# Collecting three scan directions in one order: where the third direction's products are put back into image order

## The reference

```python
y_f = mamba_dir(xz, ...)                                   # pixels in order
y_b = flip(mamba_dir(flip(xz, -1), ...), -1)               # pixels backwards
xz_s = xz.reshape(b, 2*D_INNER, NSLICES, m).swapaxes(-1, -2).reshape(b, 2*D_INNER, l)
y_s = mamba_dir(xz_s, ...)                                 # third direction: pixels in sliced order
y_s = y_s.reshape(b, D_INNER, m, NSLICES).swapaxes(-1, -2).reshape(b, D_INNER, l)
y = y_f + y_b + y_s
```

## Time and profile before

| what | value |
|---|---|
| median of three runs | 746.49 us |
| the profiled execution, span | 750.81 us, 749.0 us |
| scan layer, six tiles | 298.3 to 601.1 us of the span |
| busy share of the whole span | TensorE 81%, VectorE 86%, ScalarE 68%, GpSimd 57% |
| mean granted TensorE clock | 0.935 |

### The profile page before, as it was taken

One profiled execution on the slowest core, in us unless ns is written; L12 is line 12 of the kernel. 1 busy time (PEld: TensorE's weight loads), 2 busy tenths in 40 slices (PEclk: granted clock), 3 DMA queues, 4 the chain that ended last, 5 costly groups with the idle time before them and its releaser, 6 DMA issues.

```text
span 749.0 us, 11674 instructions
## 1 busy us (share of the span) xinstructions
PE 609.9 (81%) x3947; PEld 349.8 (47%) x3947; DVE 647.5 (86%) x896; ACT 509.2 (68%) x608; POOL 427.3 (57%) x292
## 2 busy tenths in 40 slices
PE   7899998999988952577776777776757888799997
PEld 5655546677764310244443544454435653233332
DVE  7798996889976979999999899999998874788876
ACT  2658531879976767697886796888868611477673
POOL 3699993000001075798898798798986911533331
PEclk9999999999999985699998797999987999999999
DMA  2004200331001031000000000000000013100000
GB/s 58 4 13 97 37 1 8 71 95 24 4 3 60 14 84 39 1 1 0 1 1 0 1 0 1 0 1 1 0 1 0 1 46 56 42 1 0 15 1 14
DMA packets 28853, 14.98 MB, mean 20 GB/s; under 512 B 23022, under 2 KB 24942, under 8 KB 28654
## 3 DMA queue, kind: packets, MB, share of 16 engines
q1 hardware_dynamic: 27582, 13.61, 8.2%
q10 hardware_dynamic: 1216, 0.66, 0.4%
HBM read 5.14 MB, written 0.78 MB: 8 GB/s over the span
## 4 chain that ended last, share of the span: by engine, by line
PE 38%; DVE 36%; ACT 11%; issue 9%; POOL 4%; DMA 0%; DVEq 0%; SPq 0%; ACTq 0%; POOLq 0%
PE ps L588 35%; DVE arena L1397 15%; DVE ps L1069 8%; ACT arena L1639 3%; DVE arena L1069 3%; DVE arena L1115 2%; POOL arena L1800 2%; ACT arena L1753 2%; DVE ps L1115 1%; DVE arena L1284 1%; PE ps L649 1%; PE ps L770 1%; DVE arena L1348 1%; ACT arena L1740 1%; ACT ps L1740 1%
## 5 line engine op out<-in xcount | busy, mean ns | idle before, releaser
L588 PE MATMUL ps<-arena 128*32 128x64 f32 (+5 forms) x2072 | 338.4, 352 | 110.9 <-ACT arena L1753 33.6
L588 PEld LDWEIGHTS ps<-arena 128*32 128x32 f32 (+4 forms) x2072 | 123.4, 123 | 243.4 <-issue 96.2
L1800 POOL TENSOR_TENSOR arena<-arena 128x1024 f32<-128x1024 f32 x91 | 181.7, 2011 | 33.1 <-DVE arena L1397 14.4
L1397 DVE TENSOR_TENSOR_SCAN arena<-arena,ps 128x1024 f32<-128x1024 f32 x60 | 137.2, 2287 | 8.2 <-DVE ps L1069 0.5
L1785 ACT ACTIVATE arena<-ps,nycol 128x1024 f32<-128x1024 f32 x64 | 71.2, 1115 | 56.9 <-PE ps L588 56.9
L1069 DVE TENSOR_TENSOR ps<-arena,ps 128x1024 f32<-128x1024 f32 x69 | 83.8, 1214 | 9.0 <-PE ps L588 8.3
L1397 DVE TENSOR_TENSOR_SCAN arena<-ps,arena 128x1024 f32<-128x1024 f32 x36 | 81.6, 2267 | 0.1
L1740 ACT ACTIVATE arena<-arena,a_col 128x1024 f32<-128x1024 f32 x60 | 68.7, 1144 | 10.1 <-DVE arena L1397 9.7
L1924 POOL TENSOR_TENSOR arena<-arena,bmask 128x128 f32<-128x128 f32 x64 | 30.9, 485 | 77.9 <-PE ps L588 66.8
L1069 DVE TENSOR_TENSOR arena<-ps,arena 128x512 f32<-128x512 f32 (+2 forms) x75 | 48.6, 654 | 24.5 <-PE ps L588 19.7
L1639 ACT ACTIVATE arena<-arena 128x256 f32<-128x256 f32 x128 | 59.0, 504 | 6.1 <-DVE arena L1284 4.7
(11 more groups left out here) (209 smaller groups left out, 1021.0 us busy)
## 6 DMA issues: line engine op xcount, KB each, us to landing
arena<-arena SPq DMA_DIRECT2D x54, 64.0 KB
arena<-arena SPq DMA_DIRECT2D x12, 128.0 KB, 3.3
w_conv<-in_c_far SPq DMA_DIRECT2D x1, 1152.0 KB, 5.7
w_conv<-rpb_pad SPq DMA_DIRECT2D x36, 28.0 KB, 1.8
arena<-x SPq DMA_DIRECT2D x12, 64.0 KB, 2.0
arena<-x1t SPq DMA_DIRECT2D x12, 64.0 KB, 2.0
arena<-x3t SPq DMA_DIRECT2D x12, 64.0 KB, 2.0
arena<-arena SPq DMA_DIRECT2D x2, 288.8 KB, 3.7
```

Source lines behind the costliest of these rows:

```text
L588: return pe.matmul(o, l, r, start=start, stop=stop, **k)
L1397: ve.tensor_tensor_scan(hs_ring[n % RING], decay, add, 0.0, ALU.mult, ALU.add).then_inc(S("scan"), 1)
L1800: return gp.tensor_tensor(o, a, b, ALU.mult)
```

## The change

GpSimd's products of the third direction are written in image order. The states and C are read in sequence as before, and the output is addressed so that neighbours in the sequence land 64 elements (256 bytes) apart. All three directions of a pair then add up in one sum. `turn_back` at the tile changes 0 to 1 and 3 to 4, `collect_third` and both ScalarE copies for them are gone, and so are two items of the ring (102 items are left of 104). The skip term of tiles 0 and 3 is written in image order as well, by ScalarE, with a read in steps of 16 elements. The counts of the semaphores `y_turned` and `y_back` follow. No wait is added.

```diff
 ITEMS = [(k, what) for k in range(DP) for n in range(NS)
-         for what in ["third"] * (k % DIRS == 1 and n == 0) + ["skip"] * (n == SKIP_AT) + [n]]
+         for what in ["skip"] * (n == SKIP_AT) + [n]]
...
                 collect(hc_ring[item(k, n) % RING], first=(k % DIRS == 0 and n == 0),
-                        last=(k % DIRS != 1 and n == NS - 1), halves_of=end)
+                        last=(k % DIRS == DIRS - 1 and n == NS - 1), halves_of=end)
...
-            def collect_third(k):
-
-                p = k // DIRS
-                pe.wait_ge(S("y_natural"), p + 1)
-                collect(hc_ring[item(k, "third") % RING], first=True)
...
-                    if k % DIRS == 1 and n == 0:
-                        pe.wait_ge(S("y_turned"), 1 + 2 * (k // DIRS))
-                        turn_back(ORDER[k - 1], 6)
                     if k * NS + n + AHEAD < DP * NS:
                         spread(*divmod(k * NS + n + AHEAD, NS))
-                    if k % DIRS == 1 and n == 0:
-                        collect_third(k)
...
-                    if n == 3 and k in (1, DIRS, DIRS + 1):
+                    if n == 3 and k == DIRS:
                         ac.wait_ge(S("y_acc"), above(item(k - 1, NS - 1) + 1))
-                        copy_y(0 if k == DIRS else ORDER[k - 1], slice(0, T))
-                    if n == 4 and k % DIRS == 1:
-                        q = item(k, "third")
-                        ac.wait_ge(S("y_back"), 2 * (k // DIRS + 1))
-                        ac.wait_ge(S("y_acc"), above(q - RING + 1))
-                        ac.activation(hc_ring[q % RING].rearrange("p (s m) -> p s m", s=SLICES),
-                                      bank2(6).rearrange("p (m s) -> p s m", s=SLICES), ACT.Copy).then_inc(S("y_natural"), 1)
+                        copy_y(0, slice(0, T))
...
-                        ac.activation(hc_ring[q % RING], u[:, t // PAIRS, t % PAIRS, ::step], ACT.Copy,
+                        to, of = hc_ring[q % RING], u[:, t // PAIRS, t % PAIRS, ::step]
+                        if k % DIRS == 0:
+                            to, of = to.rearrange("p (s m) -> p s m", s=SLICES), of.rearrange("p (m s) -> p s m", s=SLICES)
+                        ac.activation(to, of, ACT.Copy,
                                       scale=d_col[:, t // PAIRS, t % PAIRS:t % PAIRS + 1]).then_inc(S("skip"), 1)
...
-                    mul(hc_ring[item(k, n) % RING], hs_ring[n % RING][:, ::step], c_ring[n % RING][:, ::step]).then_inc(S("hc"), 1)
+                    to, state, c = hc_ring[item(k, n) % RING], hs_ring[n % RING][:, ::step], c_ring[n % RING][:, ::step]
+                    if k % DIRS == 0:
+                        to = to.rearrange("p (s m) -> p m s", s=SLICES)
+                        state, c = (v.rearrange("p (m s) -> p m s", s=SLICES) for v in (state, c))
+                    mul(to, state, c).then_inc(S("hc"), 1)
```

More of the change, by code:

```diff
@@ L923, in collect_state @@
                 if k == DIRS and n == 0:
-                    pe.wait_ge(S("y_turned"), 2)
+                    pe.wait_ge(S("y_turned"), 1)
                 collect(hc_ring[item(k, n) % RING], first=(k % DIRS == 0 and n == 0),
-                        last=(k % DIRS != 1 and n == NS - 1), halves_of=end)
+                        last=(k % DIRS == DIRS - 1 and n == NS - 1), halves_of=end)
             def collect_skip(k):
@@ L973, in _ @@
                             mm(ps[:, h, :], w_out[:, 0], u[:, 0, 0, HALF * h:HALF * h + HALF], start=True, stop=False)
-            turn_back(1, 4, halves_ready=4)
+            turn_back(1, 4, halves_ready=2)
             for h in range(2):
@@ L1410, in _ @@
                     if k == DP - 1 and n == NS - 1:
-                        ve.wait_ge(S("y_back"), 6)
+                        ve.wait_ge(S("y_back"), 2)
                         gate(0, slice(0, T))
@@ L1421, in _ @@
             for h in range(2):
-                ve.wait_ge(S("y_back"), 7 + h)
+                ve.wait_ge(S("y_back"), 3 + h)
                 gate(1, slice(HALF * h, HALF * h + HALF))
```

## The result

The changed kernel takes 750.62 us, the median of six runs (750.08 to 752.07); the kernel before, on the same chip, 746.38 us (744.54 to 747.54). The ratio is 1.0057, with a 95% interval of 1.0037 to 1.0076, which lies above 1: 4.2 us slower. The changed kernel is slower, by about half a per cent.

A forecast was written before the change was run, and what follows sets the result against it. VectorE's scans and injections were taken to bound the scan layer. On the profiled execution 750.81 - 1.84 + 2.84 + 0 (GpSimd) + 0 (ScalarE) = 751.8 us; that +1.0 us set on the median gave 747.5 us, range 743.5 to 762.

The forecast's parts named there:

- the first rival: GpSimd bounds tiles 0 and 3: from 2.23 us per product, costing 3.7 us at 2.58; slower, chance 0.28.
- The case that the prediction gave most of the chance: Whole kernel: time the same within half a per cent, 3.7 us; chance 0.63.
- GpSimd's write: Tiles 0 and 3: 32 products written in 256-byte steps stay at 1.96 us each, adding 0; dear end 3.78 us.
- The removal: Tiles 1 and 4: dropping transposes and ScalarE copies, which lay in a gap, saves at most 1.84 us of VectorE waits.
- The uncovered gap: Tiles 1 and 4: TensorE idles longer, its clock drops, VectorE waits; net +1.0 us taken, between -1.84 and +2.15.
- The skip term: ScalarE, tiles 0 and 3: strided read takes 1.15 us, at most 1.9, covered by room; 0, uncovered 1.5 us at most.
- The second rival: Tiles 1, 2, 4 and 5: the clock stays up and 5.8 us of waits go, 740.7 us; faster, chance 0.09.

The follow-up runs named there:

- write_only: Kernel before with GpSimd's third-direction products written in 256-byte steps, the turning left in: 748.96 us, ratio 1.0007.
- turn_removed: Changed kernel with plain addresses for the products and the skip term, so the third direction is added in wrong order: 746.57 us, ratio 0.9984.
- before2: The kernel before, unchanged, run and profiled once more: 747.57 us, ratio 1.0015; its profiled execution took 745.33 us.
- filled: Changed kernel, skip term read in sequence and written in 256-byte steps, plus 16 zero transposes before the late spread of tiles 1, 2, 4, 5: 750.92 us, 1.0064.
- skip_read: turn_removed with only the skip term's read in steps of 64 bytes put back in tiles 0 and 3: 750.74 us, ratio 1.0064.
- skip_longer: turn_removed with two short plain ScalarE activations ahead of the skip term in tiles 0 and 3, no stride: 750.4 us, ratio 1.0063.
- skip_pool: Changed kernel with the skip terms of tiles 0 and 3 made by GpSimd at state 14 instead of ScalarE: 748.23 us, ratio 1.0010.
- after2: The changed kernel, unchanged, run and profiled once more: 750.84 us, ratio 1.0039.

## Why the prediction was right, and where it was wrong

The time of 750.62 us lies in the range of 743.5 to 762 us. The forecast of 747.5 us is 3.1 us too low, and its own upper end, 750.1, is passed by 0.5 us. That the time is inside the range all the same is luck: the range reached to 762 us for the first rival, which did not come about. The case that the prediction gave most of the chance, within 0.5%, is the one that the point value of 1.0057 just misses.

**GpSimd's write: right.** 1.96 us was taken and 1.96 was measured; `write_only` shows no cost in time either. The first rival with its 2.23 and 2.58 us per product did not come about. The rule of the Trainium skill that stood against it (GPSIMD Engine Reference, section 7) is one for reads, and on this chip it doesn't carry over to this write.

**The removal: right.** "The turning lay in a gap". `spread(1, 4)` stands in after at 359.56, again 9.43 us behind its tile's first scan at 350.13, and `turn_removed` has a ratio of 0.9984 with 1 in its interval.

**The uncovered gap: right in kind, its price not settled.** TensorE's timeline of after shows the gap of tile 2 in tile 1, to the number of the earlier trace rows:

```profile
359.56 1.04 PE L588 MATMUL ps<-arena 96*128 96x512 bf16 x4 [3.32 <-DVE arena L1386]
```

The clock of tiles 1 and 4 fell from 0.96 and 0.97 to 0.90 in both. The four matmuls still took 1.04 us, and the clock fell behind them: it was 0.76 from 359.5 to 361.5 us and 0.50 in the 2 us after that. No wait of 0.97 us followed there; the one wait comes later, 0.77 us in tile 1 and 0.73 in tile 4. With the 0.48 us that stayed (a scan behind VectorE's own injection, which stands in every trace here, with the turning and without) that is 1.98 us, against 1.84 in the first trace of before: +0.14 us, where I took +1.0. But that trace is a long execution. In `before2` the two tiles have

```profile
363.45 1.23 DVE L1069 TENSOR_TENSOR ps<-arena,ps 128x1024 f32<-128x1024 f32 x1 [0.16 <-PE ps L588]
378.71 1.23 DVE L1069 TENSOR_TENSOR ps<-arena,ps 128x1024 f32<-128x1024 f32 x1 [0.16 <-PE ps L588]
510.58 2.29 DVE L1397 TENSOR_TENSOR_SCAN arena<-arena,ps 128x1024 f32<-128x1024 f32 x1 [0.48 <-DVE ps L1069]
```

0.80 us in all, and against these after is at +1.2 us and `turn_removed`, with 0.81 + 0.48 = 1.29 us, at +0.5. So the traces put the term anywhere from about nothing to the +1.0 us and a little more, and which of them is right isn't shown. The median of `turn_removed` gives no sign of it, and `filled` shows waits that move between tiles.

**The skip term: this step failed.** I set it at nothing: 1.15 us for the strided read, "if the strided read of line 1749 ... is the measure", 1.9 us at most, and up to 0.75 us "covered" by ScalarE's room. Each of the three parts was off. The measure was wrong: line 1749 reads PSUM, where the step of 64 bytes costs nothing (1.00 us), and the skip term reads SBUF, where it takes 2.05 us. The upper bound, from VectorE's line 1079, was passed by 0.15 us. And the cover was not there. ScalarE's idle time in a tile is no room for it at state 8, because the copy of C, for which TensorE waits with VectorE right behind it, stands only one decay further on. "Uncovered it would be 1.5 us at most" counted ScalarE's own microseconds, but the longer idle time that they gave to TensorE had the 1.2 GHz level behind it (0.50, above), which added to them: 2 x 1.82 us of waits at places where `turn_removed` has 0 and 0.88 us, so +2.8 us in the profiled executions. `skip_read` and `skip_longer` show that this makes the loss; `skip_pool` gets back 2.4 us of about 4. The right sum from the rows at hand was to take the dear end, 1.9 us, and to follow the copy of C behind it.

The Trainium skill has a rule that I should have weighed at this step: Advanced Engine Details and Errata, section SBUF Cachelines, says that SBUF has cachelines of 16 bytes, and that accesses which each fall in a different line pay a penalty. ScalarE's 2.05 us agrees with it, GpSimd's 1.96 us for the write does not show it.

**The second rival: fell.** In after VectorE still waits 7.1 us, and the clock in no tile is above 0.93.

**What stays open.** The profiled executions place only a part of the loss in the scan layer. Its six tiles take 301.71 us in after and 301.98 in `after2`, 298.36 in `turn_removed`, 298.69 in `before2`. From there to the end of the span it is 148.98 us in both executions of changed, and 146.23 and 146.28 in `turn_removed` and `before2`: 2.7 us more, in a layer that the change doesn't touch. TensorE's timeline shows where the two courses part, at a wait for the GpSimd line that makes its stationary operand. In after:

```profile
638.74 0.60 PE L588 MATMUL ps<-arena,w_attn 96*128 96x512 bf16 x2
642.06 2.08 PE L588 MATMUL ps<-arena 128*128 128x512 f32 x2 [2.72 <-POOL arena L1914]
643.92 1.06 PE L588 MATMUL ps<-arena,w_attn 96*128 96x512 bf16 x2
```

and in `turn_removed`:

```profile
636.84 1.06 PE L588 MATMUL ps<-arena,w_attn 96*128 96x512 bf16 x2
639.22 1.12 PE L588 MATMUL ps<-arena 128*128 128x512 f32 x2 [1.32 <-POOL arena L1908]
640.18 0.60 PE L588 MATMUL ps<-arena,w_attn 96*128 96x512 bf16 x2
```

The idle time is 2.72 us in the one and 1.32 in the other, with half the clock's speed behind the longer one (2.08 against 1.12 us for the same two matmuls). The first trace of the kernel before, at 750.81 us, has the long wait as well, 2.73 us (147.95 us from the scan layer to the end), and so has `skip_pool`'s, 2.72 us (149.17 us). Nor is the wait all of it. `write_only`, with the short skip term, has the short wait,

```profile
643.64 2.07 PE L588 MATMUL ps<-arena 128*128 128x512 f32 x2 [1.33 <-POOL arena L1928]
```

and still takes 149.19 us: in the 12 us that start 36 us behind the scan layer its granted clock is 0.50, where after has 0.72 and `turn_removed` 0.76. So the long course is not made by the skip term alone. What the longer skip term seems to do is to shut out the shorter executions: the kernel before has some at 744.4 to 745.3 us in each group, `turn_removed` has five of twelve below 745, and changed has none below 748.27. But `skip_pool`, where ScalarE has no such work, has none below 746.26, so this is not shown to be the skip term's doing alone. Why an execution takes the one or the other course at this layer wasn't tried, and I leave it open.

## What to carry to other kernels

Price a strided access by a row of the same engine and the same memory; a row from PSUM says nothing on SBUF, nor one engine's row on another's. Free time of an engine covers nothing when the next instruction in its order is one that the bounding chain waits for: look at what stands behind the place, not at the busy share. When one kernel's executions spread by more than the effect, let medians of many runs decide whether it is there, and traces only where it comes from.

## What the runs showed of the hardware

- A product on GpSimd that writes 1024 float32 in each partition with a step of 256 bytes goes at the pace of one with a plain write, 1.96 us from start to start.
- ScalarE's activation of the same size takes 1.15 us with plain addresses in SBUF, 2.03 to 2.06 us with a read in steps of 64 bytes, and 2.09 to 2.24 us with a write in steps of 256 bytes. From PSUM, the read in steps of 64 bytes takes 1.00 us, like the plain copies there (1.01 to 1.03 us).
- One kernel's executions fall on several levels of time, along with their mean granted clock: in `before2` 744.4 to 745.3 us at 0.946, 746.3 at 0.939, 747.4 to 751.7 at 0.933 to 0.937, 752.4 at 0.928. With 0.9 us more of ScalarE in two tiles the first two of these no longer came up in the 18 executions of changed.
